# A graph network kernel with 66 more gathers on GpSimd behind its last scatter

## The reference

```
# layer 0
agg = segment_sum(edge_weight[:, None] * x[src], dst)
h   = relu((x + agg) @ W1 + b1)
x   = layernorm(x + h @ W2 + b2)
# layer 1
h1  = x @ lin1_w.T
c   = 0.5 * (cos(edge_weight * pi / 10) + 1)
s   = softplus(edge_attr @ nn_w1.T + nn_b1) - log 2
W   = (softplus(s @ nn_w2.T + nn_b2) - log 2) * c[:, None]
agg = segment_sum(W * h1[dst], src)
x   = layernorm(x + (h1 + agg) @ lin2_w.T + lin2_b)
```

## Time and profile before

| | us |
|---|---|
| median of 2 runs | 9342.51 (9341.18 to 9343.85) |
| span of the profiled execution | 9314.2 |
| block 4, from GpSimd's first scatter to its first instruction behind the block | 4569.5 to 9213.3 |
| of it behind the start of the last scatter | 449 |
| median less span | 28.3 |

### The profile page before, as it was taken

One profiled execution on the slowest core, in us unless ns is written; L12 is line 12 of the kernel. 1 busy time (PEld: TensorE's weight loads), 2 busy tenths in 40 slices (PEclk: granted clock), 3 DMA queues, 4 the chain that ended last, 5 costly groups with the idle time before them and its releaser, 6 DMA issues. The chain is left out here.

```text
span 9314.2 us, 204001 instructions
## 1 busy us (share of the span) xinstructions
PE 6033.2 (65%) x35189; PEld 4808.1 (52%) x35190; DVE 6494.6 (70%) x20428; ACT 3471.8 (37%) x6781; POOL 6297.2 (68%) x6541
## 2 busy tenths in 40 slices
PE   2666666666666666666655556666666666666676
PEld 1444444444444444444444446666666666666665
DVE  7777777777777776665655556777777777777655
ACT  2333333333333333333544443333333333333202
POOL 2777777777777777775277777777777777777400
PEclk8676766776767667776855557888888888888887
DMA  3444444444444444444444446666666666666554
GB/s 101 148 146 147 148 144 146 149 146 143 146 149 147 145 145 148 149 147 142 143 134 134 134 134 199 208 210 206 205 206 208 209 207 206 205 207 207 174 167 147
DMA packets 803241, 1533.30 MB, mean 165 GB/s; under 512 B 193070, under 2 KB 206820, under 8 KB 802707
## 3 DMA queue, kind: packets, MB, share of 16 engines
q1 hardware_dynamic: 593415, 1093.58, 36.2%
q0 software_dynamic: 209456, 436.16, 15.7%
q10 hardware_dynamic: 348, 3.33, 0.1%
HBM read 967.92 MB, written 564.58 MB: 165 GB/s over the span
## 5 line engine op out<-in xcount | busy, mean ns | idle before, releaser
L1204 POOL DMA_INDIRECT sorted_messages<-rows,sidx x3224 | 3212.4, 996 | 1154.7 <-issue 932.4
L432 POOL DMA_INDIRECT xg<-x_rows,gidx x3224 | 3043.0, 944 | 1306.8 <-issue 1020.2
L475 PE MATMUL bank<-onehot,xg 128*128 128x42 f32 x6448 | 1116.6, 326 | 1400.4 <-DMA xg<-x_rows,gidx 1386.2
L475 PEld LDWEIGHTS bank<-onehot,xg 128*128 128x128 f32 x6448 | 1004.2, 233 | 1474.0 <-DMA xg<-x_rows,gidx 1457.1
L1132 PE MATMUL bank<-hot,block_rows 128*128 128x128 f32 x9312 | 1576.2, 347 | 145.4 <-DVE hot L1286 145.1
L1132 PEld LDWEIGHTS bank<-hot,block_rows 128*128 128x128 f32 x9312 | 1530.3, 260 | 169.2 <-issue 154.0
L481 PE MATMUL bank<-attr,nn 128*128 128x512 f32 x1612 | 1453.7, 1057 | 3.0 <-DVE hid L506 3.0
L1102 PE MATMUL bank<-w_nn2T,e_hid 128*128 128x128 f32 x6448 | 1039.0, 314 | 162.2 <-DMA e_hid<-hidden 162.1
L1102 PEld LDWEIGHTS bank<-w_nn2T,e_hid 128*128 128x128 f32 x6448 | 1007.8, 226 | 245.3 <-DMA e_hid<-hidden 212.1
L1113 PE MATMUL bank<-h1w,ohT 128*128 128x128 bf16 x3224 | 349.4, 275 | 1069.6 <-DVE ohT L1233 1066.4
L1257 DVE SCALAR_TENSOR_TENSOR rows<-filt,meta,bank 128x128 f32<-128x128 f32 x3224 | 904.7, 343 | 94.7 <-DVE filt L1248 47.2
(11 more groups left out here) (180 smaller groups left out, 7427.8 us busy)
## 6 DMA issues: line engine op xcount, KB each, us to landing
block_rows<-sorted_messages SPq DMA_DIRECT2D x389, 792.0 KB
hidden<-hid SPq DMA_DIRECT2D x404, 512.0 KB
e_hid<-hidden SPq DMA_DIRECT2D x403, 512.0 KB
sorted_messages<-zero SPq DMA_DIRECT2D x403, 264.0 KB
dstb<-dst SPq DMA_DIRECT2D x403, 256.0 KB
attr<-attr_cols SPq DMA_DIRECT2D x403, 204.0 KB
xg<-x_rows,gidx POOLq DMA_INDIRECT x3224, 4.2
sorted_messages<-rows,sidx POOLq DMA_INDIRECT x3224
```

What stands on the lines that cost most here:

```text
L432: pool.indirect_dma_start(xg[s][:, :], None, x_rows, bass.IndirectOffsetOnAxis(ap=gidx[s // HALF][:, s % HALF:s % HALF + 1], axis=0),).the ...
L475: nc.tensor.matmul(bank[0][:, 0:WIN], xg[s][:, :], onehot[:, s, :], start=(s == 0), stop=(s == SUB - 1)).then_inc(summed, 1)
L1204: pool.indirect_dma_start(table, bass.IndirectOffsetOnAxis(ap=sidx[b][h][:, s:s + 1], axis=0), rows[b][h][:, s, :], None).then_inc(landed[ ...
```

## The change

`layer1_edges` gets three more arguments: `x_rows`, `srci` (which it doesn't use) and `wgt` under the name `unread`. At the start of block 4 GpSimd writes the numbers 0 to 127 into a new tile `row_numbers`, one for each partition. Behind its last scatters and its four waits for `landed` it issues 66 gathers, six of each of eleven shapes (rows x numbers), with a wait for the landing of all six behind each shape. Rows of 16 and 64 numbers are parts of rows of x, those of 512 numbers are four rows of x in one. The six of a shape go side by side into the columns of `wgt`. Nothing reads what they bring.

```
@@ layer1_edges @@
+    row_numbers, numbered, extra_in = sbuf("row_numbers", [P, 1], i32), sem("row_numbers_set"), sem("extra_in")
...
         @block.gpsimd
         def _(pool):
             jobs = TileTable(pool, "pool1", nwin)
+            pool.iota(row_numbers[:, :], pattern=[[0, 1]], base=0, channel_multiplier=1).then_inc(numbered, 1)
...
             for b in range(2):
                 for h in range(2):
                     pool.wait_ge(landed[b][h], room(sent.number(b)))
+            pool.sem_inc(numbered, 1)
+            pool.wait_ge(numbered, 2)
+            issued = 0
+            for rows_of, width in ((128, 128), (64, 128), (32, 128), (16, 128), (120, 128), (127, 128), (124, 128), (112, 128),
+                                   (128, 16), (128, 64), (128, 512)):
+                table_of = x_rows.rearrange("n (a w) -> (n a) w", w=width) if width < D else x_rows.rearrange("(n a) w -> n (a w)", a=width // D)
+                for k in range(6):
+                    pool.indirect_dma_start(unread[0:rows_of, k * width:(k + 1) * width], None, table_of,
+                                            bass.IndirectOffsetOnAxis(ap=row_numbers[0:rows_of, 0:1], axis=0)).then_inc(extra_in, 16)
+                    issued += 1
+                pool.wait_ge(extra_in, 16 * issued)
```

More of the change, by code:

```diff
@@ L609, in edge_network_kernel @@
                          h1_parts, sorted_d, dstf, rank, meta, cols, basef, base, nwin, pidx, spare_rows,
-                         ones3, landed, bias3, w_sb["nn2T"], bank, aggT, slot_node, slot_row, tail)
+                         ones3, landed, bias3, w_sb["nn2T"], bank, aggT, slot_node, slot_row, tail, x_rows, srci, wgt)
         with ExitStack() as c6:
@@ L979, in layer1_edges @@
 def layer1_edges(nc, sem, sbuf, dst16, hid_d, h1_parts, sorted_d, dstf, rank, meta, cols, basef, base, nwin,
-                 pidx, spare_rows, ones3, landed, bias3, nn2T, bank, aggT, slot_node, slot_row, tail):
+                 pidx, spare_rows, ones3, landed, bias3, nn2T, bank, aggT, slot_node, slot_row, tail, x_rows, srci, unread):
     f32, i32, i16, bf16 = mybir.dt.float32, mybir.dt.int32, mybir.dt.int16, mybir.dt.bfloat16
```

## The result

| | us |
|---|---|
| before, median of 2 | 9342.51 (9341.18 to 9343.85) |
| changed, median of 2 | 9403.44 (9397.43 to 9409.44) |
| ratio | 1.0058, 95% interval 1.0039 to 1.0077 |
| forecast | 9353, range 9339 to 9379 |

The change costs 61 us and not 10, and the time lies outside the range. It is within 2% of before. The profiled execution of the changed kernel has a span of 9407.8 us and is one of the timed ones, 9409.44: what lies around the span is 1.6 us. So the 28.3 us that I set aside for the kernel before can't be what lies around a span: its profiled execution was a short one of its kind. Over all later runs the kernel before took 9321.6 to 9365.8 us.

A forecast was written before the change was run, and what follows sets the result against it. No engine fills the span; behind the last scatter, load latency in series with VectorE and TensorE sets the pace. Terms 0 + 0 + 0 + 10.3 us on 9342.5 gave 9352.8, rounded to 9353 us, range 9339 to 9379.

The forecast's parts named there:

- the 28.3 us: Kernel before: timed median of 9342.51 us less the profiled span of 9314.2 us; left alone, forecast added to the median.
- The iota: One iota on GpSimd ahead of its first scatter, covered by a 172.01 us wait: cost 0, or 0.12 us uncovered.
- The transfer engines: In the tail, the gathers' 15.9 us of DMA time meet block loads for a share of 0.65: 10.3 us.
- rival C: In the tail, gathers fall into the engines' idle 48% or loads pass them: 9342.5 to 9345 us; chance 0.25.
- Uneven shapes: Added gathers of 127, 124 and 120 rows: taken to spread evenly over the DMA engines, like 128 rows.
- Rival A: In the tail, uneven gathers sit on one engine and delay block loads: 8 us more, 9361 us; chance 0.19.
- the pairs after 8900: Pairs of turns in the tail after the gathers' expected end near 8896 us: claimed to be as before.
- GpSimd's own time: 66 gathers behind the last scatter: eleven groups of 7.5 us plus 4.1 us landing, 128 us, covered, cost 0.
- The cover of 445 us: GpSimd's idle time between last scatter and last stage: hides the gathers' 128 us, 317 us stay.
- Rival D: Behind the last scatter, uneven gathers take 2.4 us per row and outlast GpSimd's cover: 10,855 us; chance 0.02.
- E: Rival for the block's end: the 66 gathers aren't made; time within 9340 to 9345 us; chance 0.01.
- Rival B: In the tail, longer pauses keep TensorE at 1.2 GHz: 2.0 us a pair, 26 us, 9379 us; chance 0.07.

The follow-up runs named there:

- e1_after_again: The changed kernel once more, unaltered, beside the kernel before on the same chip; 9397.4 us, ratio to before 1.0059.
- e2_iota_late: The changed kernel with the iota moved from ahead of the scatters to right ahead of the gathers; 9358.9 us, ratio to before 1.0014.
- i1_only_127: As h4_act_no_uneven, with the shape of 127 rows put back and 120 and 124 left at 128; 9359.1 us, ratio to before 1.0014.
- h2_f32_then_act: The whole change, with its iota in f32 and ScalarE turning the numbers into int32; 9357.4 us, ratio to before 1.0015.
- h4_act_no_uneven: As h2_f32_then_act, with the shapes of 120, 127 and 124 rows replaced by 128 rows; 9342.6 us, ratio to before 1.0001.

## Why the prediction was wrong

**The iota: the step that failed.** "Cost 0. If that cover were gone it would be 0.12 us." I priced the instruction and its cover and nothing else. It did run under its cover, in 0.14 us. What it cost was 11 ns for each of the 3224 scatters behind it, 35 us, and 38.5 us by the times of `e1_after_again` and `e2_iota_late`. Every number for the price was in the rows except the one that counts, and that one isn't in the trace of before: the only int32 result of GpSimd in it is a memset of one column in the setup block (L215). I should have seen that the iota's form was new (all four in the setup block write f32), and that it stands ahead of the engine that paces the stage: between two scatters GpSimd mostly idles for 0.30 us and no more, so a ns on every scatter puts some 3 us on the time.

**The transfer engines: a term too large.** I took 10.3 us for 69.9 units of even gathers, with 0.65 of their DMA time paid. Even gathers cost 3 to 5 us of tail (452.1 and 453.6 against 448.6) and nothing that the times can tell from the scatter of the runs. So rival C was nearer for even gathers, and 0.65 was too high a share.

**Uneven shapes: the wrong choice, with the right rival beside it.** I took "even spreading, the nearest row". Rival A names what happened; it put 8 us on top of mine. Over even gathers the three shapes cost 11 us of tail (463.8 against 452.9). Its reason, loads held up beside the gathers, accounts for some 5 us where it stands alone (`i1_only_127`, 459.0 against 453.6). Most of the 11 us comes after the gathers, from the order of the waits that slipped by one turn, which no rival had: the prediction took it that the pairs after 8900 would be as before. For GpSimd's own time I had said that no row shows anything else than 0.94 us, and "fewer rows may need less time": 16 rows take 0.84, 127 take 2.54.

**What was right.** The cover of 445 us was not used up: the gathers took 127 us for a forecast of 128. That it came so near was luck: GpSimd was busy for 77.6 us instead of 62, and ten waits for a landing were 27.1 us in all instead of 41. Rival D fell with that, E too. Rival B had the right price, some 2 us for a pair, and the wrong place: beside the gathers the granted clock was 0.82, as in the same 127 us of before, but in the late tail it was 0.84 with the mixed gathers and 0.85 without, as fewer pairs ran at full clock.

**The sum in the end.** 38 us for the int32 iota and 13 for the gathers (`h2_f32_then_act`) are 51 of the 57 us of `e1_after_again`; the difference is within what the runs scatter.

**The yardstick.** I compared the median with the span of an execution that was itself some 27 us shorter, and called the difference what lies around it. The sum didn't suffer, as it was added to the median; but the range of 2.7 us for "runs of before differ" came from two runs, and 26 runs later gave 44 us.

## What to carry to other kernels

An instruction that runs in idle time can still cost, if it changes how fast later instructions of its engine run: look at whether its form (operation and types) is new to the program, and how many instructions of a pacing engine come behind it. Ahead of a loop of scatters on GpSimd, let another engine turn numbers into int32 (`h2_f32_then_act`), or do it behind the loop (`e2_iota_late`). Where anything else waits on the DMA engines, avoid a gather of 127 rows; 16, 32, 64, 112 and 128 rows together cost 5 us of tail (`h4_act_no_uneven`). Where two buffers are filled and used in turn and one load of each pair is waited for, look at which one: if it changes, the loop has slipped into its other order, and the slower pairs say nothing of the loads.

## What the runs showed of the hardware that I had not expected

- An int32 result that GpSimd computes (an iota, or a copy from f32) makes every later scatter to DRAM 11 ns longer, 965 instead of 954 ns at least, until the end of the stage, over 4450 us and 3224 gathers. Gathers aren't touched (938 ns). A f32 iota, a memset of an int32 tile and a semaphore increment don't do it; an affine_select, a memset and DMAs don't undo it. What it is inside GpSimd stays open.
- A gather of 127 rows keeps GpSimd for 2.54 us at least, one of 124 rows for 1.28, one of 128 rows for 0.94, one of 16 rows for 0.84.
- The loop of the tail over its two buffers has two orders that last. After a disturbance (six gathers each of 120, 127 and 124 rows, or 66 of 127) the wait moved to the load of the other buffer and stayed there to the end of the block, some 300 us in the first case, with GpSimd idle. A pair then takes 10.16 to 10.21 us instead of 9.98 to 10.08, with loads as quick as ever (4.4 to 4.6 us from issue to landing).
- A pair of turns in which TensorE's granted clock stays at 1.00 takes 8.40 us, one in which it is 0.83 in the mean 9.90.
- In this kernel the DMA engines of the tail were 52% busy, and 4 MB of even gathers thrown in cost 3 to 5 us of tail.
